# A cross-attention and FFN kernel: maxima turned in fp32, FFN slices cut at whole pieces, values projected behind the queries, and a value pair moved

## The reference, cut to what matters

```python
x = x + xattn(layernorm(x), ctx, ctx)      # 16 heads x 4 "superposed" parts, dk = 8
x = x + ffn(layernorm(x))                  # 4-bit weights, 512 -> 2 x 1376 -> 512

def xattn(q, k, v):
    proj = lambda x, W, b: (x @ W.T + b).reshape(b, s, H, dk, M).transpose(0, 2, 1, 3, 4)
    interfere = lambda x: x + 0.1 * amp * einsum('bhsdi,hij->bhsdj', x, interference)
    scores = einsum('bhqdm,bhkdm->bhqkm', qh, kh) / sqrt(dk)
    out = einsum('bhqkm,bhkdm->bhqdm', softmax(scores, axis=3), vh)
    return out @ Wo.T + bo

def ffn(x):                                # W = scale[group] * (nibble - zero[group])
    gate, up = split(x @ w_gu)
    return (silu(gate) * up) @ w_d
```

## Time and profile before

| | us |
|---|---|
| median of 3 runs | 938.86 |
| lowest, highest | 938.69, 940.80 |
| the profiled execution, its own time | 941.57 |
| its span, from first to last instruction | 939.80 |
| mean granted TensorE clock | 0.891 of full |

### The profile page before, as it was taken

The page is one execution under the profiler, slowest core; times in us unless marked ns, Lnnn a source line. Parts: engine busy times, 40 slices in busy tenths (PEclk is TensorE's granted clock), DMA queues, the critical chain, the costliest instruction groups (busy, mean ns, idle before and its releaser), DMA issues.

```text
span 939.8 us, 23081 instructions
## 1 busy us (share of the span) xinstructions
PE 757.6 (81%) x9441; PEld 530.1 (56%) x9441; DVE 550.0 (59%) x1141; ACT 429.2 (46%) x806; POOL 324.5 (35%) x290
## 2 busy tenths in 40 slices
PE   5405566666998899889988988898889989999798
PEld 5303322221577467746774777477647764776485
DVE  7987765655566456645764576357635763556421
ACT  1326466656355345534462446254526442654220
POOL 6643155425224412431243125212621352144211
PEclk9757655555899999999999999999999999999999
DMA  8900232121010020002000200020002000100000
GB/s 244 296 1 1 59 80 61 53 68 54 23 28 2 13 63 22 2 13 73 13 2 13 84 1 3 20 75 1 3 27 69 2 2 24 26 2 3 24 1 23
DMA packets 20702, 36.97 MB, mean 39 GB/s; under 512 B 3374, under 2 KB 7602, under 8 KB 20592
## 3 DMA queue, kind: packets, MB, share of 16 engines
q1 hardware_dynamic: 20604, 35.48, 13.0%
HBM read 26.56 MB, written 4.19 MB: 33 GB/s over the span
## 4 chain that ended last, share of the span: by engine, by line
issue 46%; PE 19%; POOL 14%; DVE 12%; ACT 6%; DMA 2%; SPq 1%; POOLq 0%; ACTq 0%; DVEq 0%
POOL arena L1357 8%; PE bank L513 4%; POOL arena L1344 3%; PE bank L528 3%; PE bank L494 2%; PE bank L484 2%; PE bank L445 2%; POOL arena L1335 2%; PE bank L448 2%; DMA arena<-in_L_xattn_Wo 2%; PE bank L446 2%; DVE arena L973 2%; DVE arena L1082 1%; ACT arena L776 1%; DVE nmf L1154 1%
## 5 line engine op out<-in xcount | busy, mean ns | idle before, releaser
L513 PE MATMUL bank<-arena,WGU 128*128 128x256 f16 (+1 forms) x2112 | 250.3, 275 | 8.5 <-DVE arena L1130 7.1
L513 PEld LDWEIGHTS bank<-arena,WGU 128*128 128x128 f16 (+1 forms) x2112 | 205.2, 101 | 36.7 <-DVE arena L1130 9.0
L1357 POOL TENSOR_TENSOR arena<-arena 128x512 f16<-128x512 f32 x128 | 145.0, 1161 | 207.8 <-ACT arena L855 207.8
L528 PE MATMUL bank<-WD,arena 128*128 128x512 f16 (+1 forms) x528 | 125.7, 387 | 9.3 <-DVE arena L1130 9.3
L484 PE MATMUL bank<-arena,WT 128*128 128x256 f16 x768 | 91.8, 280 | 40.4 <-DVE arena L708 39.2
L1344 POOL TENSOR_TENSOR arena<-arena 128x512 f16<-128x512 f32 (+1 forms) x48 | 51.6, 1075 | 207.9 <-ACT arena L828 207.9
L484 PEld LDWEIGHTS bank<-arena,WT 128*128 128x128 f16 x768 | 76.6, 100 | 56.0 <-issue 43.2
L848 ACT ACTIVATE arena<-bank,small 128x512 f32<-128x512 f32 x128 | 77.6, 688 | 36.9 <-PE bank L643 36.8
L494 PE MATMUL bank<-WT,arena 128*128 128x512 f16 x384 | 89.0, 387 | 1.8 <-DVE arena L706 1.8
L1154 DVE TENSOR_REDUCE nmf<-bank 128x8 f32<-128x512 f32 x128 | 81.5, 683 | 14.4 <-PE bank L617 14.4
L1106 DVE SCALAR_TENSOR_TENSOR arena<-arena,small 128x512 f16<-128x512 f32 x64 | 45.3, 749 | 70.8 <-ACT arena L812 70.8
(11 more groups left out here) (161 smaller groups left out, 1062.8 us busy)
## 6 DMA issues: line engine op xcount, KB each, us to landing
arena<-in_L_ffn_qweight_gu SPq DMA_DIRECT2D x8, 688.0 KB, 5.6
arena<-arena SPq DMA_DIRECT2D x32, 144.0 KB, 2.6
WT<-in_ctx SPq DMA_DIRECT2D x8, 512.0 KB, 15.2
arena<-in_ctx SPq DMA_DIRECT2D x8, 512.0 KB, 3.5
arena<-in_x SPq DMA_DIRECT2D x8, 512.0 KB, 3.6
out_y<-arena SPq DMA_DIRECT2D x16, 256.0 KB, 2.1
arena<-in_L_ffn_qweight_down SPq DMA_DIRECT2D x10, 256.0 KB, 3.4
arena<-in_L_xattn_Wk SPq DMA_DIRECT2D x1, 1024.0 KB, 5.9
```

Of the source, the lines that this page charges most:

```text
L513: mm = e.matmul(pb[0:m, i * TOK:(i + 1) * TOK], WGU[:, sp, kb, half * INTER + fb * P:half * INTER + fb * P + m], x2T[:, mp, kb, :], start= ...
L528: mm = e.matmul(pb[:, :], hT[0:m, sp, fb, t * P:(t + 1) * P], WD[0:m, mp, fb, :], start=(n == 0), stop=(n == 3 * FB - 1))
L1357: e.tensor_tensor(phl[:, a, 1, :], pring[:, a, :], phl[:, a, 0, :], ALU.subtract).then_inc(S["p_lo"], 1)
```

## The change

The negative maxima stay fp32: `dve_split_max` is gone, DVE writes them into a wider tile (8 of every 32 columns), PE transposes this tile in fp32, ACT copies it in fp32, and the 16 selector matmuls of a batch take fp32 operands. LIFT is no longer added to the maxima; log(P_SCALE) is the bias of the exponential. The slices end where pieces end. Value projections (from chunk 1 on) stand between slices 0 and 1, behind keys and queries; the x2 transposes stand behind the keys. In a batch the turn stands behind the first slice, the turned scores behind the second, and the second value pair behind the third. `EXTRAS` has two places in each batch, behind the turn and behind the second value pair. ACT, DVE and POOL follow in their order.

```diff
-EXTRAS = (("cT0",), ("cT1",), ("xT0",), ("xT1", "oT0"))
+EXTRAS = ((("cT0",), ("cT1",)), ((), ()), (("xT0",), ("xT1",)), (("oT0",), ()))
-PRE, EACH, TAIL = (16, 26), (20, 22, 8, 24), (16, 16, 10, 16)
+PRE, EACH, TAIL = (24, 24), (24, 6, 18, 24), (12, 16, 14, 18)
-        nmf = sb("nmf", [P, 32], F32)
-        nrest = sb("nrest", [P, 32], F32)
-        nm16 = sb("nm16", [P, 4, 4, 8], BF16)
-        nmT = sb("nmT", [P, P], BF16)
-        sel = sb("sel", [P, KB, P], BF16)
+        nmf = sb("nmf", [P, 4, 32], F32)
+        nmT = sb("nmT", [P, P], F32)
+        sel = sb("sel", [P, KB, P], F32)
...
 def pe_chunk
-            for t in range(TILES):
-                pe_rows(e, 2, t, AB[2 + t], cxT, S["proj_done"])
-                if not first and t == 0:
-                    e.wait_ge(S["y_ready"], 2 * c)
-                    for i in range(TILES):
-                        pe_transpose_tile(e, c, f"x2T{i}", xln, S["x2ln_ready"], 2 * (c - 1) + i + 1)
...
+            else:
+                e.wait_ge(S["y_ready"], 2 * c)
+                for i in range(TILES):
+                    pe_transpose_tile(e, c, f"x2T{i}", xln, S["x2ln_ready"], 2 * (c - 1) + i + 1)
             for G in range(2):
                 reached(e, S["x2_part"], 2 * c - 1 + G)
                 pe_project(e, 0, G, JB[G], xnT)
-                if not first and G == 0:
-                    e.wait_ge(S["t_lo"], t_at(c, "x2T1"))
-                ffn_slice(G)
+            if not first:
+                e.wait_ge(S["t_lo"], t_at(c, "x2T1"))
+            ffn_slice(0)
+            if not first:
+                for t in range(TILES):
+                    pe_rows(e, 2, t, AB[2 + t], cxT, S["proj_done"])
+            ffn_slice(1)
...
                 ffn_slice(slot[0])
                 if b:
                     pe_values(e, c, 2 * b - 2)
+                pe_turn_max(e, c, b)
+                pe_extras(e, c, EXTRAS[b][0])
                 ffn_slice(slot[1])
+                pe_scores_turned(e, c, b)
+                ffn_slice(slot[2])
                 if b:
                     pe_values(e, c, 2 * b - 1)
-                pe_turn_max(e, c, b)
-                pe_extras(e, c, b)
-                ffn_slice(slot[2])
-                pe_scores_turned(e, c, b)
+                pe_extras(e, c, EXTRAS[b][1])
                 ffn_slice(slot[3])
...
         def pe_turn_max(e, c, b):
-            e.wait_ge(S["nm_split"], NB * c + b + 1)
-            e.matmul(AB[0][:, 0:P], nm16[:, :, :, :].rearrange("p a k n -> p (a k n)"), ident16[:, :],
-                     start=True, stop=True).then_inc(S["nm_turned"], 1)
+            e.wait_ge(S["max_done"], SLOTS * c + 4 * b + 4)
+            e.transpose(AB[0][:, 0:P], nmf[:, :, :].rearrange("p a n -> p (a n)"), ident[:, :]).then_inc(S["nm_turned"], 1)
...
         def act_exp
-            e.activation(pring[:, a, :], AB[a][:, :], ACT.Exp, scale=KSM).then_inc(S["exp_done"], 1)
+            e.activation(pring[:, a, :], AB[a][:, :], ACT.Exp, bias=LIFT, scale=KSM).then_inc(S["exp_done"], 1)
...
 def act_chunk
+                if b:
+                    act_p_hi(e, c, 4 * b - 2)
+                    act_p_hi(e, c, 4 * b - 1)
                 act_slot(e, c, slot[0], first)
-                act_slot(e, c, slot[1], first)
                 act_copy_max(e, c, b)
-                for name in EXTRAS[b]:
+                for name in EXTRAS[b][0]:
                     if name in (T_LAST if last else T_ORDER):
                         act_hi(e, c, name)
-                act_slot(e, c, slot[2], first)
+                act_slot(e, c, slot[1], first)
                 act_exp(e, c, 4 * b)
...
+                act_slot(e, c, slot[2], first)
                 act_p_hi(e, c, 4 * b)
                 act_p_hi(e, c, 4 * b + 1)
+                for name in EXTRAS[b][1]:
+                    if name in (T_LAST if last else T_ORDER):
+                        act_hi(e, c, name)
                 act_slot(e, c, slot[3], first)
-                act_p_hi(e, c, 4 * b + 2)
-                act_p_hi(e, c, 4 * b + 3)
...
 def dve_chunk
             dve_mask(e, c, 2, 0, 0)
+            if not first:
+                dve_v(e, c, 0, 5)
+            dve_mask(e, c, 3, 0, 1)
+            if not first:
+                dve_v(e, c, 1, 6)
             dve_slot(e, c, 0, first)
-            dve_mask(e, c, 3, 0, 1)
+            if not first:
+                dve_v_lo(e, c)
             dve_slot(e, c, 1, first)
             for b in range(NB):
                 slot = IN_BATCH[b]
-                dve_max(e, c, 4 * b), dve_max(e, c, 4 * b + 1)
+                for a in range(4):
+                    dve_max(e, c, 4 * b + a)
                 dve_slot(e, c, slot[0], first)
-                dve_max(e, c, 4 * b + 2), dve_max(e, c, 4 * b + 3)
-                dve_split_max(e, c, b)
                 if b:
                     dve_o(e, c, 2 * b - 2)
+                for name in EXTRAS[b][0]:
+                    if name in (T_LAST if last else T_ORDER):
+                        dve_lo(e, c, name)
                 dve_slot(e, c, slot[1], first)
+                dve_slot(e, c, slot[2], first)
                 if b:
                     dve_o(e, c, 2 * b - 1)
-                for name in EXTRAS[b]:
+                for name in EXTRAS[b][1]:
                     if name in (T_LAST if last else T_ORDER):
                         dve_lo(e, c, name)
-                dve_slot(e, c, slot[2], first)
```

More of the change, by code:

```diff
@@ L462, in pe_transpose_tile, with pe_extras @@
             mm.then_inc(S["tr_done"], 1)
-        def pe_extras(e, c, b):
-            for name in EXTRAS[b]:
+        def pe_extras(e, c, names):
+            for name in names:
                 if name not in (T_LAST if is_last(c) else T_ORDER):
@@ L871, in act_chunk @@
                              pring[:, 2 + t, :].rearrange("p (h q n) -> p h q n", h=HEADS, q=2), ACT.Copy).then_inc(S["v_hi"], 1)
+        def act_chunk(e, c, first=False, last=False):
+            act_qk(e, c, 0, 1, 0)
             if first:
+                act_whi(e, 2)
+            else:
+                act_hi(e, c, "x2T0"), act_hi(e, c, "x2T1")
+            act_qk(e, c, 1, 1, 1)
+            if first:
+                act_whi(e, 3)
+                act_scale_part(e, 1)
+                act_v_hi(e, c)
                 e.wait_ge(S["wlo_done"], 3)
@@ L1182, in dve_apply_next, with dve_v, dve_v_lo @@
                 ln_apply(e, "x", c + 1, t, xin[:, t, :], S["xln_ready"])
+        def dve_v(e, c, t, turn):
+            e.wait_ge(S["proj_done"], 6 * c + turn)
+            reached(e, S["p_lo"], SLOTS * c - 1 + t)
+            e.scalar_tensor_tensor(pring[:, 2 + t, :], AB[2 + t][:, :], KV, bv_row[:, :], ALU.mult, ALU.add).then_inc(S["v_evicted"], 1)
+        def dve_v_lo(e, c):
+            for t in range(TILES):
+                e.wait_ge(S["v_hi"], 2 * c + t + 1)
+                e.tensor_tensor(ap(vsb[:, t], 0, P, 18, [(VROW, HEADS), (HEADS * VROW, 2), (1, 16)]),
+                                pring[:, 2 + t, :].rearrange("p (h q n) -> p h q n", h=HEADS, q=2),
+                                ap(vsb[:, t], 0, P, 0, [(VROW, HEADS), (HEADS * VROW, 2), (1, 16)]), ALU.subtract).then_inc(S["v_lo"], 1)
         def dve_chunk(e, c, first=False, last=False):
@@ L1193, in dve_chunk @@
                 dve_wlo(e, 3)
[L1194 to L1205 removed]
+                dve_v(e, c, 0, 3), dve_v(e, c, 1, 4)
+                dve_v_lo(e, c)
                 dve_lo(e, -1, "xT0"), dve_lo(e, -1, "xT1")
```

66 lines of the change are left out of this document (20 added, 46 removed).

## The result

Four runs of the changed kernel took 908.09 to 909.98 us, median 908.44; the kernel before took 938.78 on the same chip (937.53 to 940.8). The ratio is 0.9678, 95% interval [0.9658, 0.9698]: 30.3 us faster. The forecast was 901 in 892 to 941, so the sign and the range held and the point was 7 us too low. The profiled execution took 908.39 us, span 906.7, against 941.57 and 939.80 before.

A forecast was written before the change was run, and what follows sets the result against it. PE bounds the kernel. Removing its waits (59.7 us) and low clock (6.4) gives -66.1; new waits +7.6, fp32 +19.0 and chunk 0 +1.8 make -37.7, so 901 us from the 938.86 median; range 892 to 941.

The forecast's parts named there:

- 1.5 us wait at oT0: PE's oT0 transpose waits for DVE to empty its bank; standing alone removes this and, with it, the low clock.
- keys-queries-values: Projections in this order, chunks 1 to 7: scores of batch 0 lose their mask wait of up to 1.7 us.
- Whole pieces: Gate or up pieces ending with their slice remove bank waits: down projection 1.3 us, a gate piece 1.0.
- The late second pair: Second value pair behind 24 units and turned scores, over 4 us of cover, loses its wait of up to 1.7 us.
- The new wait: PE's earlier turn waits for DVE's maxima: 0.2 us in batch 0, 1.0 in batch 1, none later; sum 7.6.
- nearest form: Selector matmuls on PE: four fp32 row groups overlap as in bf16, 0.85 us per batch, 0.63 more than bf16.
- s: Extra PE time per batch for fp32 selectors and turn: 0.68 us, making 19.0 over 28 batches.
- +5.4 for fp32, -3.6 for the splits: Chunk 0 at half clock: fp32 costs 5.4 us, four splits of 0.9 leave its serial chain; net +1.8.
- A: Selector matmuls: only one row group advances at a time, 1.70 us per batch, total 932; chance 0.20.
- B: Selector matmuls: fp32 loads of 32 rows don't overlap, 3.4 us per batch, total 993, slower; chance 0.19.
- C: Turn: maxima late in all four batches, 1.3 us each, new waits 36.4 instead of 7.6, total 930; chance 0.15.
- D: PE's waits stay where they are under other names, total 938 to 941; chance 0.04.

The follow-up runs named there:

- e3: Changed kernel with DVE's statistics and layernorm of the next x moved ahead of the third slot in chunks 1 to 6: 895.47 us, ratio 0.9549.
- e1: Changed kernel with its maxima split in three bf16 parts again and no bias in the exponential, new order kept: 907.0 us, ratio 0.9674.
- e5: Changed kernel with the second value pair back behind the second slice, ahead of the turned scores: 922.55 us, ratio 0.9842.
- e2: Kernel before with fp32 maxima alone; order, slices and value projections as before: 950.77 us, ratio 1.0143.
- e4: Changed kernel with value projections back behind the key projections and the x2 transposes between them: 907.97 us, ratio 0.9679.
- e6: Changed kernel with eight units shifted from the first slice to the last, so pieces end inside the next slice: 918.65 us, ratio 0.9798.
- e7: Changed kernel with 16 extra zero-weight fp32 matmuls of 32 rows per batch, in four forms; run once for its trace: 971.51 us.
- e11: e9 with chunk 0's batches in the order of before: 890.31 us, ratio 0.9497.
- e9: e3 with the maxima split in bf16 parts again: 894.15 us, ratio 0.9528.
- e8: e3 with the batches of chunk 0 alone in the order of before on PE, ACT and DVE: 893.73 us, ratio 0.953.
- e12: e11 with the transposes cT0, xT0 and oT0 ahead of the turn in batches 0, 2 and 3: 879.42 us, ratio 0.9371.
- e10: e3 with LIFT added in ACT's copy of the turned maxima instead of as the exponentials' bias: 895.38 us, ratio 0.9545.

## Why the prediction was right, and where it was wrong

**What bounds the kernel: right.** PE's 59.7 us of waits and the 6.4 of low clock in chunks 1 to 7 were the prize, and all of it went: the time is PE's own work plus its waits, and e3, with no wait at the turn, gains what the rows of waits say. What makes the clock fall is less clear than I put it. Removing the 1.5 us wait at oT0 was to remove it, and in e1, whose turn waits 1.73, it is back. But e5 shows it with no wait over 1.1 us, the same as the change, which doesn't; and e2 keeps waits of 1.7 and 1.5 us without it. It stays open.

**Which edit removes which wait: partly wrong, partly not shown.** I gave keys-queries-values the 1.7 us before the scores; e4 shows that it brings nothing, which leaves the two slices behind the queries. Whole pieces held (e6: 14.7 us of waits come back without them). The late second pair held, but it isn't alone: the 18.1 us go by the pair's new place (e1) and just as well by dropping the split (e2); with the split gone, the old place brings 5.1 back (e5). No run puts oT0 back beside xT1, or takes back the cover of the tail's first pair, so that the 9.0 and 4.4 us went by those edits is the forecast's argument only.

**The new wait: 10.2 us for 7.6.** Batch 1 waits 1.09 where 1.0 was worked out, by the chain given; e3, which takes DVE's own work out of it, removes it. Batch 0 waits not at all for the 0.2 foreseen. Batch 2's 0.61 was ruled out by 3.2 us of cover against 3.1: a margin of 0.1 us carried a "nothing". Two terms were missing in it: the exponentials' bias (+0.36 us for four), and the two applies, together 1.84 us, that stand in DVE's list not far ahead of those maxima.

**fp32 on PE: the mechanism right, the size not.** The term was 16 x 0.212 / 4 = 0.85 for the selectors and 0.11 for the turn; they measured 1.08 and 0.16. The overlap of four row groups is as assumed (e7). What the bound of "nearest form" left out is the change between f16 and fp32, some 0.06 us per group, of which a batch has four. That makes s = 0.96, and 7.9 us more than forecast: by itself the size of the miss.

**Chunk 0: the step that failed.** The forecast had "+5.4 for fp32, -3.6 for the splits", net +1.8, and called itself wrong if chunk 0 moved by more than 5 us; it moved by 5.5. What the ledger put at nothing, without a reason, is the order, which costs 5.0 us there with the split and 2.3 with fp32 (e11's table). Its fp32 part was not far off for the old order: with the measured s it would be 8 x 0.96 - 3.6 = +4.1, and 3.2 was measured (e2). PE's timeline of the kernel after shows the start of the order's loss, PE idle between the first scores and the first turn:

```profile
107.79 1.47 PE L619 MATMUL bank<-arena 32*128 32x128 f16 x48 [4.39 <-DVE arena L1118]
111.81 0.48 PE L629 MATMUL bank<-ident,nmf 128*128 128x128 f32 x1 [2.56 <-DVE nmf L1166]
```

In chunk 0 there is no FFN to hide the maxima, and the second slice, whose two parts of dequantization stood ahead of the first turn, now stands behind it. So the turn waits 2.56 us, and 3.6 in e1, where the old order had no such wait. How the rest of the 5 us of e1 is spread over dequantization I have not separated.

**Why the sum still came within 7 us.** The errors in cost add to 14.2: fp32 +7.9, chunk 0 +3.7, waits +2.6. Against them stands what I hadn't counted: 43 waits fewer also save their drained tails, about 6.9 us. That the two cancel by half is luck. A forecast that had both would have said 908, and that it then meets the median is luck again: against the profiles, where the saving was 33.1 us for the 37.7 forecast, the same corrections give 30.4, which is 2.7 too little (the ends' 1.1 and the 1.6 unexplained).

**The rivals.** A and B are out by e7. C's four late batches did not come (two did, 10.2 us of its 36.4), and D is out, since the six rows of waits are gone. (The low end of the range, 892, was to be the forecast without the new waits; 901 less 7.6 is 893.) "Faster" was right, but not for the reason that the form of the forecast suggests: whether maxima turn in fp32 or in bf16 parts is no matter in the new order (e1 against the change, e9 against e3), and a loss in the old one (e2) or when only chunk 0's order is restored (e8 against e11: 0.0033 of 938, 3 us).

## What to carry to other kernels

Cost the parts of a change in each other's presence: fp32 cost 13 us in the old order and nothing in the new, because in the new one the split that it replaces stands on the wait. Where an order makes a wait, move what stands ahead of it on the late engine (e3, 13 us) and put ready work of the waiting engine in front of it (e12, 11 us) before paying for shorter work. And cost the new order separately in the stage that lacks the old cover, here the first chunk.

## What was not expected of the hardware

- fp32 matmuls of 32 rows (e7): some 0.105 us a record in one row group, four row groups abreast, and 64 moving columns no cheaper than 128. 64 stationary columns were dearer, 0.38 us for eight records against 0.22 to 0.28. The Trainium skill (TensorE: Matmul & The Clock Gate, section LDWEIGHTS) gives a weight load a time by its columns whatever the rows are, 107 ns for 128. The trace agrees on that number for a record of 128 columns. For 64 the same rule gives half, and the matmuls came no sooner, so a load's time alone does not set the pace. And loads of different row groups overlapped, which the section does not say: the 3.4 us per batch estimated from it did not come, and 1.08 was measured.
- The bias operand on an exponential of 128x512 from PSUM: 777 ns for 688, and gone again when the bias is taken off (e10).
- A granted clock above half in chunk 0: a mean of 0.54 for 0.50, in three stretches of some 3.5 us at 2.4 GHz that the kernel before has not. The fp32 kernels e2, e3 and e10 have three as well (0.54), e4 two (0.53) and e8 one (0.51); the split ones e1, e9 and e11 have none (0.50).
